# TensorE of a fused attention and expert kernel in periods of two slots

## The chip, the cores and the metric

The kernel runs on one core of one Trainium2 chip. The metric is the device time of that core in microseconds (us), the median of several executions. The profile is one further execution, taken by the hardware profiler; times in it count from the span's start.

## The reference, cut to what matters

The input x is [8, 256, 128] in float32. It is normalised over its last axis. One branch is causal attention with 16 heads of 64: queries from x, keys and values through a latent of 64, rotary positions, softmax, output projection. The other branch is a feed-forward network of 8 experts (128 to 512 to 128, GELU) of which each token takes one, and a SiLU behind it. The result is x plus attention times gate:

```python
q = q * cos + _rotate_half(q) * sin
k = k * cos + _rotate_half(k) * sin
scores = einsum('bhsd,bhtd->bhst', q, k) / sqrt(D) + causal
probs = softmax(scores)
out = einsum('bhst,bhtd->bhsd', probs, v)
s = out.reshape(B, S, H * D) @ wo.T
g = silu(2 * expert_of_token(xn))
return x + s * g
```

## The kernel before, in words

Attention goes by slots. A slot is a pair of heads of one batch: 8 slots a batch (NP), 64 slots in all, number g. Each engine has its own list of instructions, written out slot by slot by a function `slot(g)`, and the engines meet only at semaphores; every engine works strictly down its list. Between slots 39 and 40 (G_LEAD is 40) stands the expert phase, 22 tiles of 128 sorted tokens.

What each engine does in slot g, in its order:

- TensorE: `scores(g+2)` (two heads, each on 64 rows of the array, into one PSUM bank a head, lines 1116 and 1118); `project(m)` of one item, a group of four heads' queries (even m, lines 1090 to 1092) or keys (odd m, lines 1106 and 1107); `turn(g)`, six transposes of the probabilities (line 1128); `output(g-3)` (line 1156); in even slots `values(g-2)`, which serves two slots and has 64 columns of the array a head (lines 1142 and 1144). Slots 0 to 23 and a few others (ALONE) have a values step of their own.
- VectorE: `row_max(g+2)` (masks the scores and takes the row maximum, four instructions, line 602), `denominators(g+1)` (the reciprocals `rden`, line 609), its share of `scale(g+1)` (line 620), then sometimes `finalise` of a batch (lines 784 to 790), then `rotate(m)` (the products of the rotary rotation, line 593).
- ScalarE: the exponentials of g+1 (line 906), a copy of the context (`ctx_out`, line 935), the copies of the turned probabilities (`turned_probs(g)`, line 928), its share of `scale(g+1)` (line 919).
- GpSimd (POOL): its share of `scale(g+1)` (line 477), then the sum that ends a rotation (`rotated(m)`, line 466, into `staged`), then in slots 22 to 37 one `scatter` of 128 tokens to DRAM by expert (line 485), and in slots 43 to 58 one `gather` (line 493).
- SyncE starts transfers: `place(n)`, four moves from `staged` to `qk_sb` (line 366), when both items 2n and 2n+1 are summed; `store` of a finished batch; and in slot 38, once all scatters have landed, the loads of the sorted tokens into `z` (line 428). It also works down one list, and a wait in it holds back all that follows.

`items(g)` is the item projected, rotated and summed in slot g, g+6 up to slot 36, and TWICE puts a second one into slots 36 and 38, so that item 45 belongs to slot 38 and from slot 39 on it is g+8. Scores of a slot wait for their moves (`qk_in`) and for both heads' maxima of the slot before (`masked_ready`).

SyncE's slot, the lines that matter:

```python
if g == G_LEAD - 2:
    sp.wait_ge(scattered, 16 * NT)
    load(0, 4)
    sp.wait_ge(xs_in, 16)
    load(4, NR)
for m in items(g):
    if m % 2:
        place(m // 2)
```

TensorE ends attention before the experts with `output`, `values(39)`, a wait for the first load of `z` (`xs_in` 16), the first transpose of a tile of tokens (line 1297), `output(39)`; it waits for the second load (`xs_in` 32) before the second product of tile 1 (line 1339).

## Time and profile before

| | us |
|---|---|
| median of 3 runs | 305.51 (305.35 to 305.71) |
| the profiled execution, its own time | 305.23 |
| its span from first to last instruction | 303.5 |
| TensorE busy | 290.1 (96% of the span) |
| ScalarE busy | 243.2 (80%) |
| VectorE busy | 227.1 (75%) |
| GpSimd busy | 217.2 (72%) |

The profiled execution's time is its span and 1.7 us around it. Busy time of TensorE is modelled from pipelined matmuls, and a busy engine may also be one that works no faster than its supply comes. The shares are means over stages that have different limits.

### The profile page before, as it was taken

What the parts mean: (1) busy time and instruction counts of PE and PEld (TensorE: products, weight loads), DVE (VectorE), ACT (ScalarE), POOL (GpSimd) and SP (SyncE); (2) the same over time, 40 slices, a digit from 0 to 9 for tenths busy, and PEclk for the clock granted to TensorE, in tenths of its full rate; (3) what the DMA queues carried; (4) which work ended last, traced back from release to release, by engine and by line L of the source; (5) the groups of instructions that cost most, each with busy time, mean ns of one, the idle gap of its engine ahead of it and who ended that gap; (6) DMA issues with size and microseconds to landing.
All of it is one profiled execution on the core that took longest, in us unless ns stands there. A gap on an engine that the chain in (4) does not pass through costs nothing.

```text
span 303.5 us, 8596 instructions
## 1 busy us (share of the span) xinstructions
PE 290.1 (96%) x2362; PEld 234.8 (77%) x2362; DVE 227.1 (75%) x905; ACT 243.2 (80%) x871; POOL 217.2 (72%) x321
## 2 busy tenths in 40 slices
PE   8897999999999999999999999999999999899994
PEld 3665888888888888777777789999877777676763
DVE  4889998987786998988888524444398899897651
ACT  4387889898977789989898677777779989799982
POOL 3468878687777779999999963333158999899730
PEclk9999999999999999999999999999999999999999
DMA  6854594979433333333334490000513344344200
GB/s 203 251 132 116 104 297 116 236 172 303 101 68 65 67 77 83 101 88 98 89 88 109 96 288 6 2 2 0 154 38 83 100 120 117 93 115 123 61 19 17
DMA packets 39596, 33.35 MB, mean 110 GB/s; under 512 B 4801, under 2 KB 36674, under 8 KB 39554
## 3 DMA queue, kind: packets, MB, share of 16 engines
q1 hardware_dynamic: 38098, 30.51, 39.1%
q0 software_dynamic: 1024, 2.10, 2.5%
q8 instruction: 20, 0.33, 0.5%
q10 hardware_dynamic: 432, 0.23, 0.3%
q14 instruction: 22, 0.18, 0.2%
HBM read 11.07 MB, written 4.98 MB: 53 GB/s over the span
## 4 chain that ended last, share of the span: by engine, by line
PE 66%; POOL 12%; issue 8%; DVE 6%; DMA 3%; ACT 2%; SPq 2%; POOLq 1%; DVEq 0%; ACTq 0%
PE bank L1128 9%; PE bank L1116 9%; PE bank L1142 8%; PE bank L1339 7%; PE bank L1156 6%; PE bank L1327 6%; POOL probs L477 4%; POOL staged L466 4%; PE bank L1090 4%; PE bank L1144 3%; PE bank L1118 3%; DVE masked L602 2%; PE bank L1106 2%; POOL xn L493 2%; DMA z<-in_woT 2%
## 5 line engine op out<-in xcount | busy, mean ns | idle before, releaser
L906 ACT ACTIVATE pexp<-masked,negmax 128x128 f32<-128x128 f32 (+1 forms) x256 | 114.1, 453 | 2.2 <-DVE negmax L602 2.2
L477 POOL TENSOR_SCALAR probs<-pexp,rden 128x256 f32<-128x256 f32 (+1 forms) x184 | 80.3, 451 | 24.3 <-DVE rden L609 21.7
L602 DVE CUSTOM_DVE_ANT_0 masked<-bank,mask 128x128 f32<-128x128 f32 (+1 forms) x256 | 75.9, 352 | 25.2 <-PE bank L1118 25.0
L466 POOL TENSOR_TENSOR staged<-rot_out 128x512 f32<-128x512 f32 x63 | 80.1, 1273 | 17.5 <-DVE rot_out L593 16.9
L593 DVE TENSOR_TENSOR rot_out<-bank,rot 128x1024 f32<-128x1024 f32 x64 | 77.6, 1214 | 3.9 <-PE bank L1092 2.7
L928 ACT COPY probsT<-bank 128x384 f32<-128x384 f32 x128 | 55.0, 481 | 23.8 <-PE bank L1128 22.8
L1128 PE MATMUL bank<-ident,probs 128*128 128x128 f32 x384 | 54.1, 275 | 1.3 <-POOL probs L477 0.6
L906 ACT ACTIVATION_READ_ACCUMULATOR pexp<-masked,negmax 128x1 f32 x256 | 50.0, 195 | 0.0
L1116 PE MATMUL bank<-qk_sb 64*128 64x256 f32 x256 | 45.0, 427 | 3.2 <-DVE negmax L602 2.5
L1128 PEld LDWEIGHTS bank<-ident,probs 128*128 128x128 f32 x384 | 43.1, 140 | 4.1 <-issue 1.5
L1156 PE MATMUL bank<-vo_sb,ctxT 128*128 128x128 f32 x256 | 39.5, 279 | 0.7 <-ACT ctxT L935 0.7
L1142 PE MATMUL bank<-probsT,lat_all 128*64 128x256 f32 (+1 forms) x184 | 37.7, 488 | 0.3 <-ACT probsT L928 0.3
L1156 PEld LDWEIGHTS bank<-vo_sb,ctxT 128*128 128x128 f32 x256 | 33.6, 191 | 2.0 <-ACT ctxT L935 1.1
L1074 ACT ACTIVATE probsT<-bank,w_own 128x128 f32<-128x128 f32 x88 | 25.0, 369 | 12.7 <-PE bank L1327 12.7
L1116 PEld LDWEIGHTS bank<-qk_sb 64*128 64x128 f32 x256 | 19.4, 184 | 17.0 <-issue 14.2
L551 POOL COPY w_own<-w_sb 128x516 f32 x22 | 14.9, 678 | 23.1 <-ACT probsT L1074 22.9
L1118 PEld LDWEIGHTS bank<-qk_sb 64*128 64x128 f32 x256 | 25.1, 187 | 2.6
L935 ACT COPY ctxT<-bank 128x256 f32<-128x256 f32 (+1 forms) x46 | 20.7, 451 | 6.0 <-PE bank L1144 5.1
L1118 PE MATMUL bank<-qk_sb 64*128 64x128 f32 x256 | 25.0, 270 | 0.0
L885 DVE TENSOR_TENSOR z<-bank,b_all 128x128 f32 (+1 forms) x22 | 6.4, 292 | 24.2 <-PE bank L1339 21.7
L1144 PEld LDWEIGHTS bank<-probsT,lat_all 128*64 128x64 f32 x184 | 13.3, 137 | 14.3 <-issue 10.3
L1339 PE MATMUL bank<-w_sb,probsT 128*128 x176 | 23.3, 276 | 0.3 <-ACT probsT L1074 0.3
(114 smaller groups left out, 485.6 us busy)
## 6 DMA issues: line engine op xcount, KB each, us to landing
qk_sb<-staged SPq DMA_DIRECT2D x128, 128.0 KB, 2.7
w_sb<-in_w SPq DMA_DIRECT2D x2, 1024.0 KB, 6.1
w_sb<-in_w SPq DMA_DIRECT2D x4, 512.0 KB, 4.8
sorted_x<-z SPq DMA_DIRECT2D x1, 1408.0 KB, 8.0
sorted_g<-z SPq DMA_DIRECT2D x1, 1152.0 KB, 5.9
out<-res SPq DMA_DIRECT2D x8, 128.0 KB, 1.9
x_sb<-in_x SPq DMA_DIRECT2D x3, 256.0 KB, 3.3
rot<-in_c_rot SPq DMA_DIRECT2D x1, 512.0 KB, 5.8
```

Source lines behind the costliest of these rows:

```text
L466: pool.tensor_tensor(staged[:, n % 2, :, m % 2, :], rot_out[:, m % 2, :, 0:S], rot_out[:, m % 2, :, S:2 * S], op=ALU.add).then_inc(staged_ ...
L477: pool.tensor_scalar(probs[:, g % 2, i, c], pexp[:, g % 2, i, c], rden[:, g % 2, i, k:k + 1], 1.0, ALU.mult, ALU.mult).then_inc(probs_read ...
L593: dve.tensor_tensor(rot_out[:, m % 2], bank_of(m)[:].unsqueeze(1).broadcast_to([P, 2, 2 * S]), rot[:], op=ALU.mult).then_inc(rope_done, 1)
L602: t = dve.tensor_tensor_reduce(masked[:, g % 2, i, c], s_bank[i][:, c], mask[:, c], -1.0, -NEG * 1e8, ALU.add, ALU.min, negmax[:, g % 2, i ...
L906: e = act.activation(pexp[:, g % 2, i, c], masked[:, g % 2, i, c], ACT.Exp, bias=negmax[:, g % 2, i, k:k + 1], scale=-1.0, accum_out=rowsu ...
L928: act.copy(probsT[:, g % 4, i, :], t_bank[i][:, 0:SW]).then_inc(probsT_ready, 1)
L1116: pe.matmul(s_bank[i][:, P:SW], qk_sb[r, 0, p, P:S], qk_sb[r, 1, p, :], start=True, stop=True)
L1118: m = pe.matmul(s_bank[i][:, 0:P], qk_sb[r, 0, p, 0:P], qk_sb[r, 1, p, 0:P], start=True, stop=True)
L1128: t = pe.transpose(t_bank[i][:, k * P:(k + 1) * P], probs[:, g % 2, i, k * P:(k + 1) * P], ident[:])
L1142: pe.matmul(o[r, :, :], lat_all[:, 2 * b, :], probsT[:, pairs, i, 0:S], start=True, stop=False)
L1156: m = pe.matmul(y_bank[:, i * C:(i + 1) * C], ctxT[:, p, i * P:(i + 1) * P], vo_sb[:, p, :], start=(p == 0 and i == 0), stop=(p == NP - 1) ...
L1339: m = pe.matmul(bank[6 + i][:, 0:C], hidT[:, i, k, :], w2_sb[:, k, :, :].rearrange("p e c -> p (e c)")[:, bass.ds(e * C, C)], start=(k == ...
```

## The change

In slots 26 to 37 and 42 to 57 TensorE writes two slots as one period s (s even): `scores(s+2)`, `values(s-2)`, `scores(s+3)`, `turn(s)`, one projection, two outputs, `turn(s+1)`, the next projection. In these slots VectorE does the rotation of slot g-1's items, ahead of `denominators(g+1)`, and GpSimd sums them in slot g; ScalarE copies the context in even slots after both exponentials. TWICE moves from slots 36 and 38 to 22 and 24, so `items(g)` is g+8 from slot 25 on. SyncE's list is left as it was, but it follows `items(g)`. `staged_ready` becomes one semaphore for each parity of item, scores wait for each head's maxima by itself, and the finish of batch 5 goes from slot 51 to slot 50. The sums, scalings and moves stay on their engines.

```diff
--- before.py
+++ after.py
@@ -40,7 +40,7 @@
 
 LEAD = 5
 AHEAD = 6
-TWICE = (36, 38)
+TWICE = (22, 24)
 G_LEAD = LEAD * NP
 TURNS = ((0, 2), (2, 4), (4, 8), (8, 12), (12, 16))
 W_PARTS = NG
@@ -49,10 +49,12 @@
 SCATTER_SLOT = 22
 GATHER_SLOT = G_LEAD + 3
 GATHER_ORDER = (10, 11, 0, 1, 2, 3, 12, 13, 4, 5, 6, 7, 8, 9, 14, 15)
-FINALS = {48: 0, 51: 5, 53: 1, 54: 2, 56: 3, 59: 6, 61: 4}
+FINALS = {48: 0, 50: 5, 53: 1, 54: 2, 56: 3, 59: 6, 61: 4}
 FINAL_ORDER = tuple(FINALS.values()) + (7,)
 Z_PART = 18
 FIRST_DOUBLE = 3 * NP
+PERIODS = (*range(26, G_LEAD - 2, 2), *range(G_LEAD + 2, B * NP - 6, 2))
+SCATTERS = tuple(range(SCATTER_SLOT, SCATTER_SLOT + NT))
 ALONE = tuple(range(FIRST_DOUBLE)) + (G_LEAD - 2, G_LEAD - 1, B * NP - 2, B * NP - 1)
 
 
@@ -65,6 +67,20 @@
 
     ahead = [AHEAD + sum(t < n for t in TWICE) for n in (g, g + 1)]
     return range(g + ahead[0], min(g + 1 + ahead[1], B * NP))
+
+
+def in_period(g):
+
+    return g - g % 2 in PERIODS
+
+
+def rotations(g):
+
+    behind = items(g - 1) if in_period(g - 1) else []
+    return [*behind] if in_period(g) else [*behind, *items(g)]
+
+
+VECTOR_SUMS = ()
 
 
 def host_constants():
@@ -254,7 +270,7 @@
 
         proj_done = sem("proj_done")
         rope_done = sem("rope_done")
-        staged_ready = sem("staged_ready")
+        staged_ready = [sem(f"staged_ready{i}") for i in range(2)]
         qk_in = [sem(f"qk_in{p}") for p in range(NP)]
         scores_done = sem("scores_done")
         masked_ready = sem("masked_ready")
@@ -297,7 +313,7 @@
 
         def scaler(g, i, k):
 
-            busy = SCATTER_SLOT <= g - 1 < SCATTER_SLOT + NT or GATHER_SLOT <= g - 1 < GATHER_SLOT + NT
+            busy = g - 1 in SCATTERS or GATHER_SLOT <= g - 1 < GATHER_SLOT + NT
             if g == 0 or g >= B * NP - 3:
                 return ("vector", "pool")[i]
             return "pool" if k or not busy else ("vector", "scalar")[i]
@@ -358,7 +374,8 @@
         def _(sp):
             def place(n):
 
-                sp.wait_ge(staged_ready, 2 * n + 2)
+                for i in range(2):
+                    sp.wait_ge(staged_ready[i], n + 1)
                 wait(sp, scores_done, 2 * n + 2 - NP)
                 for pair in range(2):
                     p = 2 * (n % NG) + pair
@@ -464,7 +481,7 @@
                 for q in (2 * n - 4, 2 * n - 3) if n > 1 else ():
                     pool.wait_ge(qk_in[q % NP], 32 * (q // NP) + 32)
                 pool.tensor_tensor(staged[:, n % 2, :, m % 2, :], rot_out[:, m % 2, :, 0:S], rot_out[:, m % 2, :, S:2 * S],
-                                   op=ALU.add).then_inc(staged_ready, 1)
+                                   op=ALU.add).then_inc(staged_ready[m % 2], 1)
 
             def scale(g):
 
@@ -537,10 +554,12 @@
                     rstd(2 + g // 4)
                 if g == G_LEAD - 1:
                     first_weights()
-                for m in items(g):
-                    rotated(m)
-                if SCATTER_SLOT <= g < SCATTER_SLOT + NT:
-                    scatter(g - SCATTER_SLOT)
+                for m in rotations(g):
+                    if m not in VECTOR_SUMS:
+                        rotated(m)
+                for n in range(NT):
+                    if SCATTERS[n] == g:
+                        scatter(n)
                 if GATHER_SLOT <= g < GATHER_SLOT + NT:
                     gather(GATHER_ORDER[g - GATHER_SLOT])
 
@@ -589,9 +608,16 @@
             def rotate(m):
 
                 dve.wait_ge(proj_done, m + 1)
-                wait(dve, staged_ready, max(m - 1, 2) if m > 1 else 0)
+                wait(dve, staged_ready[m % 2], m // 2)
                 dve.tensor_tensor(rot_out[:, m % 2], bank_of(m)[:].unsqueeze(1).broadcast_to([P, 2, 2 * S]), rot[:],
                                   op=ALU.mult).then_inc(rope_done, 1)
+                if m == 1 or m in VECTOR_SUMS:
+                    n = m // 2
+                    dve.wait_ge(rope_done, m + 1)
+                    for q in (2 * n - 4, 2 * n - 3) if n > 1 else ():
+                        dve.wait_ge(qk_in[q % NP], 32 * (q // NP) + 32)
+                    dve.tensor_tensor(staged[:, n % 2, :, m % 2, :], rot_out[:, m % 2, :, 0:S], rot_out[:, m % 2, :, S:2 * S],
+                                      op=ALU.add).then_inc(staged_ready[m % 2], 1)
 
             def row_max(g):
 
@@ -744,9 +770,6 @@
                 dve.wait_ge(rot_in, 16)
                 rotate(0)
                 rotate(1)
-                dve.wait_ge(rope_done, 2)
-                dve.tensor_tensor(staged[:, 0, :, 1, :], rot_out[:, 1, :, 0:S], rot_out[:, 1, :, S:2 * S],
-                                  op=ALU.add).then_inc(staged_ready, 1)
                 normalise(1)
                 rotate(2)
                 turned_low(1)
@@ -777,6 +800,7 @@
 
             def finalise(b):
                 k = FINAL_ORDER.index(b)
+                wait(dve, res_ready, k)
                 dve.wait_ge(g_in[b], 32)
                 g2 = gate[:, 2 * b:2 * b + 2, :].rearrange("p n c -> p (n c)")
                 if b >= LEAD:
@@ -791,7 +815,7 @@
                                   op=ALU.add).then_inc(res_ready, 1)
 
             def slot(g):
-                if 0 < g // NP < LEAD and g % NP == (2 if NP * (g // NP) <= FIRST_DOUBLE else 3):
+                if 0 < g // NP < LEAD and g % NP == (2 if NP * (g // NP) <= FIRST_DOUBLE or in_period(g) else 3):
                     take_y(g // NP - 1)
                 if g in FINALS and FINALS[g] >= LEAD:
                     finalise(FINALS[g])
@@ -805,6 +829,9 @@
                     row_max(g + 2)
                 if g == G_LEAD + 1:
                     gate_rows(NR - 1, 1)
+                if in_period(g):
+                    for m in rotations(g):
+                        rotate(m)
                 if g + 1 < B * NP and g != G_LEAD:
                     denominators(g + 1)
                     scale(g + 1)
@@ -854,8 +881,9 @@
                     tile_experts()
                 if g in FINALS and FINALS[g] < LEAD:
                     finalise(FINALS[g])
-                for m in items(g):
-                    rotate(m)
+                if not in_period(g):
+                    for m in rotations(g):
+                        rotate(m)
 
             def finish(b):
                 if b == B - 1:
@@ -1036,10 +1064,12 @@
                     exponentials(g + 1, 0)
                 if g > 1 and g - 2 in ALONE and g not in (G_LEAD, G_LEAD + 1):
                     ctx_out(g - 2)
-                if g % 2 and g > 2 and g - 3 not in ALONE and g not in (G_LEAD + 1, B * NP - 1):
+                if g % 2 and g > 2 and g - 3 not in ALONE and g not in (G_LEAD + 1, B * NP - 1) and not in_period(g):
                     ctx_out(g - 3)
                 if more:
                     exponentials(g + 1, 1)
+                if g in PERIODS:
+                    ctx_out(g - 2)
                 if g == B * NP - 2:
                     ctx_out(g - 2)
                 if g == B * NP - 1:
@@ -1111,8 +1141,8 @@
 
                 p = g % NP
                 pe.wait_ge(qk_in[p], 32 * (g // NP) + 32)
-                wait(pe, masked_ready, 2 * g)
                 for i, r in enumerate(half_rows):
+                    wait(pe, masked_ready, 2 * g - 1 + i if g else 0)
                     pe.matmul(s_bank[i][:, P:SW], qk_sb[r, 0, p, P:S], qk_sb[r, 1, p, :], start=True, stop=True)
                 for i, r in enumerate(half_rows):
                     m = pe.matmul(s_bank[i][:, 0:P], qk_sb[r, 0, p, 0:P], qk_sb[r, 1, p, 0:P], start=True, stop=True)
@@ -1255,7 +1285,29 @@
                 pe.wait_ge(vo_ready, 2)
                 pe.wait_ge(lat_copied, 1)
 
+            def period(s):
+                scores(s + 2)
+                if s != G_LEAD + 2:
+                    values(s - 2)
+                scores(s + 3)
+                turn(s)
+                for m in items(s)[:1]:
+                    project(m)
+                if s - 2 not in PERIODS and s - 3 not in ALONE:
+                    output(s - 3)
+                output(s - 2)
+                output(s - 1)
+                turn(s + 1)
+                for m in items(s + 1):
+                    project(m)
+                for m in items(s)[1:]:
+                    project(m)
+
             def slot(g):
+                if in_period(g):
+                    if g in PERIODS:
+                        period(g)
+                    return
                 if g + 2 < B * NP:
                     scores(g + 2)
                 if g < 2:
@@ -1276,7 +1328,7 @@
                     turn_latents(g // 4)
                 if g == COUNT_SLOT:
                     count_tokens()
-                if g > 2 and g - 3 not in ALONE and g not in (G_LEAD, G_LEAD + 1, G_LEAD + 2):
+                if g > 2 and g - 3 not in ALONE and g not in (G_LEAD, G_LEAD + 1, G_LEAD + 2) and g - 2 not in PERIODS:
                     output(g - 3)
                 if g > 1 and g - 2 in ALONE and g not in (G_LEAD, G_LEAD + 1):
                     output(g - 2)
```

## Rows read from the trace of the kernel before

**Rows 1.** The page: busy time by engine, and the chain that ended last.

```profile
PE 290.1 (96%) x2362; PEld 234.8 (77%) x2362; DVE 227.1 (75%) x905; ACT 243.2 (80%) x871; POOL 217.2 (72%) x321
...
PE 66%; POOL 12%; issue 8%; DVE 6%; DMA 3%; ACT 2%; SPq 2%; POOLq 1%; DVEq 0%; ACTq 0%
```

**Rows 2.** Busy time of each engine in two stretches of attention.

```profile
core 0: us, PE busy (x) PEld busy (x) DVE busy (x) ACT busy (x) POOL busy (x), PEclk, DMA share, GB/s
...
132.60:160.30 27.70, 27.70 (x217) 21.59 (x217) 23.61 (x90) 25.36 (x92) 26.00 (x33) 1.00 0.37 97
...
232.20:257.90 25.70, 25.70 (x202) 19.83 (x200) 23.33 (x81) 23.82 (x89) 24.13 (x29) 1.00 0.42 106
```

**Rows 3.** Chain of waits, slots 29 and 30: start, us, what.

```profile
132.58 0.63 PE bank L1116 x4
...
134.11 0.66 PE bank L1128 x6
...
135.21 0.63 PE bank L1116 x4
...
136.06 0.31 PE bank L1090
136.38 0.12 PE bank L1091
...
138.07 1.01 PE bank L1142 x4
...
139.51 0.63 PE bank L1116 x4
```

**Rows 4.** Timeline of GpSimd, slots 28, 29 and 38: start, us, operation.

```profile
132.71 0.93 POOL L477 TENSOR_SCALAR probs<-pexp,rden 128x256 f32<-128x256 f32 x2
133.62 1.26 POOL L466 TENSOR_TENSOR staged<-rot_out 128x512 f32<-128x512 f32 x1
135.05 1.06 POOL L485 DMA_INDIRECT sorted_x<-xn,pos  x1 [0.17 <-issue]
136.15 0.93 POOL L477 TENSOR_SCALAR probs<-pexp,rden 128x256 f32<-128x256 f32 x2
...
168.44 1.62 POOL L477 TENSOR_SCALAR probs<-pexp,rden 128x128 f32<-128x128 f32 x4
170.04 2.51 POOL L466 TENSOR_TENSOR staged<-rot_out 128x512 f32<-128x512 f32 x2
```

**Rows 5.** SyncE's moves: timeline, line 366 alone, and issue to landing.

```profile
169.69 3.60 SPq L428 DMA_DIRECT2D z<-sorted_x  x2
...
L366 SPq DMA_DIRECT2D qk_sb<-staged x128: 590/608/2283, 12.2 to 278.6; - x128
...
z<-sorted_x SPq DMA_DIRECT2D x1, 256.0 KB, 2.8
z<-sorted_x SPq DMA_DIRECT2D x1, 0.5 KB, 7.0
```

**Rows 6.** Timeline of TensorE: first tile of the experts, second product of tile 1.

```profile
174.55 0.33 PE L1297 MATMUL bank<-ident,z 128*128 128x128 f32 x1
...
180.44 1.06 PE L1339 MATMUL bank<-w_sb,probsT 128*128 x8
```

**Rows 7.** Timeline of slots 42 and 43: VectorE's last mask, TensorE's turn, GpSimd's scaling.

```profile
226.75 0.82 PE L1128 MATMUL bank<-ident,probs 128*128 128x128 f32 x6
226.82 0.42 DVE L602 CUSTOM_DVE_ANT_0 masked<-bank,mask 128x256 f32<-128x256 f32 x1
...
230.73 1.00 POOL L477 TENSOR_SCALAR probs<-pexp,rden 128x256 f32<-128x256 f32 x2 [0.30 <-DVE rden L609]
```

**Rows 8.** VectorE's last step of a finish (min/median/max ns), and TensorE at slot 52.

```profile
L790 DVE TENSOR_TENSOR res<-gated,x_sb x8: 424/426/2118, 247.8 to 300.8; 128x256 f32<-128x256 f32 x8
...
259.30 0.70 PE L1116 MATMUL bank<-qk_sb 64*128 64x256 f32 x4 [1.19 <-DVE negmax L602]
```

**Rows 9.** Timeline of ScalarE, slots 29 and 30: copies of the turned probabilities.

```profile
134.53 0.86 ACT L928 COPY probsT<-bank 128x384 f32<-128x384 f32 x2 [0.43 <-PE bank L1128]
...
137.39 0.86 ACT L928 COPY probsT<-bank 128x384 f32<-128x384 f32 x2
```

**Rows 10.** Timeline of GpSimd and TensorE in slots 57 and 58.

```profile
280.14 0.94 POOL L477 TENSOR_SCALAR probs<-pexp,rden 128x256 f32<-128x256 f32 x2
280.84 0.87 PE L1128 MATMUL bank<-ident,probs 128*128 128x128 f32 x6
```

## The prediction

> **What bounds the kernel now.** I read the page first. TensorE is busy 96% of the span and the chain that ended last is 66% TensorE [rows 1], so the kernel looks bound by TensorE. Next come the stretches. In slots 29 to 36 GpSimd is busy 26.00 of 27.70 us, in slots 43 to 50 it is 24.13 of 25.70 [rows 2], and its timeline shows what the rest is: 0.17 us ahead of each scatter, no wait for anybody [rows 4]. One of its slots takes 136.15 - 132.71 = 3.44, two take 6.88. The chain gives TensorE 139.51 - 132.58 = 6.93 for two slots [rows 3]. So two engines are full at once, and TensorE has 0.05 us in two slots to win before GpSimd sets the pace. GpSimd's work from slot 22 to slot 38 is a fixed list: scalings, sums, scatters.
>
> Third, the end of that stretch. SyncE starts the load of the sorted tokens at 169.69; it lands 2.8 later, at 172.5, and only then the second load starts, which lands 7.0 later, at 179.5 [rows 5]. TensorE uses the first at 174.55 and the second at 180.44 [rows 6]. That leaves 2.05 and 0.9 us of slack. From there to 218 the expert tiles follow each other on TensorE, so what comes late here comes late at the end.
>
> **The change, part by part.**
>
> Fewer changes of the array's shape on TensorE. The first projection instruction after scores takes 0.31, its like behind it 0.12: 0.19 for a change from 64 rows to the full array. Scores behind another shape take 0.63 for their wide part; the narrow part, half as wide, takes 136.06 - 135.84 = 0.22, so 0.19 is the change. Values take 1.01 for the wide part and 139.51 - 139.08 = 0.43 for the half-wide one: 0.15 [rows 3]. Two slots have five changes now (scores, projection, scores, projection, values: 4 x 0.19 + 0.15 = 0.91), a period has four (scores, values, scores, turn: 0.72). A period is 6.93 - 0.19 = 6.74 us, and there are 14 periods, so at most 14 x 0.19 = 2.7 us. GpSimd's 6.88 leaves 14 x 0.05 = 0.7, and that only where TensorE, not GpSimd, ends the stretch. I take 0 in the sum.
>
> The second items move from slots 36 and 38 to 22 and 24. No sum stands in slot 26, and slot 38 sums items 45 and 46 as before. From slot 22 through 37 GpSimd has 17 sums in both kernels, so with no idle time it ends its last scatter and starts scale(39) at 168.44 and the sum of item 45 at 170.04, as now [rows 4]. The extra sums make it up to 2.5 us late in slots 24 to 26, which TensorE waits out and gets back by slot 38; cost 0. TensorE would reach the last turns about 1 us earlier, as slots 36 and 38 have one projection less; the next part takes this away.
>
> SyncE's list. This is the largest term. The move place(22) needs items 44 and 45. Item 45 was in slot 38, behind the loads of z. Now items(37) is 45, so place(22) stands in SyncE's slot 37, ahead of the loads; but the rotation is a slot late, so its sum is still in GpSimd's slot 38, behind scale(39). It ends at 170.04 + 2.51 / 2 = 171.30 [rows 4]. SyncE waits until then, issues four moves of 0.61 each [rows 5] and comes to the first load at 171.30 + 2.44 = 173.74 instead of 169.69: 4.05 late. It lands at 176.5, where TensorE used it at 174.55: 2.0 late. The second load starts then and lands at 176.5 + 7.0 = 183.5, where TensorE used it at 180.44: 3.1 late. If the second load takes only 6 us, with four competing moves fewer behind it, the first one decides: 2.0. I take 2.8, with 2.0 to 3.5 as bounds (the upper one for a first load slowed by the four moves ahead of it). Whoever is early before it gains nothing, and the expert phase behind has no slack on TensorE to take it back.
>
> The start of the second run of periods. In slot 42 no values step stands between scores(44) and scores(45), so scores(45) wait for VectorE's last mask, which ends at 226.82 + 0.42 = 227.24. With half the wide part and the narrow part (0.22 each) and the change of shape (0.19) turn(42) starts near 228.0 instead of 226.75 [rows 7]: 1.3 late. ScalarE has already copied the context by then (0.5 less to do), so the exponentials of 44, their reciprocals and scale(44) come 0.5 to 0.8 late; GpSimd was waiting for exactly those (0.30) [rows 7]. I take 0.5, with 0 and 1.2 as bounds.
>
> Rotation ahead of the reciprocals on VectorE. The products take 1.2 and now stand between row_max and `rden`. Behind `rden` wait GpSimd's scale and all the rest of its list. The working, by order of instructions: in a period of 6.88 the scores end 1.0 after its start, the masks 1.2 later, the products 1.2 later, so `rden(s+1)` is there at 3.6; GpSimd's scaling must end as turn(s+1) starts, at 6.74 - 0.48 - 0.66 = 5.6 and when GpSimd is full about 0.5 later (0.48 is the key projection, 0.66 from 134.11 on a turn [rows 3]), so it starts near 5.2: 1.5 us of slack where GpSimd is full. Just after slot 42, where TensorE is 1.3 behind, 0.2 to 0.4 is left. So this costs nothing while no finish stands in between. A finish is two steps of some 0.43 us, and its last step once took 2.12, beside GpSimd's work; TensorE then waited 1.19 [rows 8]. There are five finishes in slots 48 to 56. With less slack each can cost up to 0.8; or the bad one is gone and 1.2 comes back. I take 0.7, with -1.2 and +2.5 as bounds. The Trainium skill (SBUF — State Buffer, "The single rule") says that VectorE and GpSimd share one port pair as an exclusive lock, so that one of them blocks for a whole instruction. By that rule a finish beside a sum loses up to 1.3 us each time, and five would lose 6; the one long row in eight [rows 8] says it is rare.
>
> A sum owed. In slots 42 to 56 each sum is one slot later, so the sum of item 63 falls in slot 56, where GpSimd had none. It takes 1.26 [rows 4], and scale(58) stands behind it. That scaling is at 280.14 and turn(58) at 280.84 [rows 10], so they are tied. I take 0.8, with 0 and 1.3 as bounds.
>
> Waits by head: the first head's scores may start half a row_max early; -0.1. The split of `staged_ready`, the earlier finish of batch 5 and the extra wait on `res_ready`: 0, each is met long before.
>
> Sum: 2.8 + 0.5 + 0.7 + 0.8 - 0.1 = 4.7. The profiled execution takes 305.23, so 309.9; the median of the runs shown is 0.28 above it, and I predict 310.2.
>
> **Rivals.**
>
> Faster: the changes of shape decide. If TensorE alone set the pace in all 14 periods and the loads of z were not held back, 2.7 us would go: 302.8. Partly (first run as forecast here by GpSimd, second by TensorE) 304. For it speaks the 66% of TensorE in the chain; against it GpSimd without idle time, and the order of SyncE's list. It decides only if place(22) costs less than 0.9 us, that is if the sum of item 45 ends before about 168. The Trainium skill (TensorEngine Tiling (Array Packing), "Key Properties") says that a change of tiling mode drains the engine. It would make this rival's 2.7 us; it gives no price, and the trace agrees with 0.15 to 0.19 each.
>
> No change: the late load is hidden and the rest cancels. It would need TensorE to reach its first tile 2 us later than now for another reason. 305.5.
>
> Only SyncE's list costs: the first term stands, the others cancel. 308.3.
>
> ScalarE becomes the bound. values(s) now needs the copies of turn(s+1), which TensorE made just before it. ScalarE starts the copies 134.53 - 134.11 = 0.4 after a turn [rows 3, 9], the next ones 137.39 - 134.53 = 2.86 later, and they take 0.86 [rows 9]: done 4.1 after turn(s) began. TensorE comes to values(s) at 6.74 - 1.44 (values) - 0.86 (the second scores) = 4.44. That is 0.3 of slack, and the context's copy, 0.5 every second slot, is not in it; with 0.2 us lost in each of 14 periods 2.8 come on top: 313.0.
>
> **How the numbers follow.** Forecast (the late load and most of the small costs) 0.5; only the late load 0.24; ScalarE or VectorE as the bound on top 0.14; no change 0.04; faster 0.08. The likeliest case's own range is 308.8 to 311.6. The range that holds 8 in 10 takes the low bound of the first term with the rest near nothing, and the upper bounds of three of the four: 306.8 to 312.8. Within 0.2% (0.6 us, about what a measurement of this kernel can tell from no change) 0.04, faster 0.08, slower 0.88.
>
> **What would show it.** In the profile after: SyncE issues four moves between the end of GpSimd's first sum of slot 38 and the first load of z, and TensorE waits for that load ahead of its first line-1297 transpose, some 2 us. GpSimd's last scatter ends at the same time as before, within 1 us. A period takes 6.9, not 6.74. Scores(45) wait for the masks. Wrong would be: a last scatter well before 167, an expert phase that starts no later than 175, or periods of 6.7.

## The result, and the profile after

| | before | after |
|---|---|---|
| median of 4 runs, us | 305.61 (305.35 to 306.38) | 313.09 (310.41 to 316.04) |
| ratio | | 1.0211 (95%: 1.012 to 1.0303) |
| profiled execution, its own time | 305.23 | 316.04 |
| its span | 303.5 | 313.9 |

The medians differ by 7.5 us. The ratio leaves out the run of 316.04, which counts as a slow one, and by it the change costs 6.4 us. The four runs spread far more than those of before: 310.41, 311.56, 314.62 and 316.04, with mean granted clocks of 0.994, 0.993, 0.974 and 0.978. The profiled execution is the slowest of them, so its last landmarks overstate the difference by about 3 us.

The page of after, busy time and the chain by engine:

```profile
PE 296.2 (94%) x2362; PEld 240.6 (77%) x2362; DVE 227.9 (73%) x905; ACT 241.7 (77%) x871; POOL 218.4 (70%) x321
PE 68%; POOL 10%; DVE 9%; issue 7%; DMA 2%; ACT 2%; SPq 1%; POOLq 0%; DVEq 0%; ACTq 0%
```

Busy shares say nothing here: TensorE is busy for 6 us more and yet has a smaller share. The chain tells more, in order of time (start, us, what), from the last scatter to tile 1 of the experts:

```profile
168.19 1.01 POOL sorted_x L502
...
170.92 1.24 POOL staged L483
...
172.21 0.59 SPq L383
172.81 0.04 issue
172.85 0.61 SPq L383
173.46 0.04 issue
173.50 0.61 SPq L383
...
174.15 0.61 SPq L383
...
174.80 2.95 DMA z<-sorted_x
177.75 0.14 issue
177.89 0.45 PE bank L1349
```

GpSimd's sum of item 45, four moves issued by SyncE, the load of `z`, the first transpose of a tile: one chain, without a gap. The first load starts at 174.80 where it started at 169.69 [rows 5]. TensorE's own timeline for the same place (the brackets give the idle time ahead of a group and what ended it) and two stretches (busy time and count of TensorE, its weight loads, VectorE, ScalarE and GpSimd; then the granted clock):

```profile
177.89 0.45 PE L1349 MATMUL bank<-ident,z 128*128 128x128 f32 x1 [3.25 <-DMA z<-sorted_x]
...
179.19 1.92 PE L1379 MATMUL bank<-probsT,w_own 128*128 128x128 f32 x8
...
185.20 1.06 PE L1391 MATMUL bank<-w_sb,probsT 128*128 x8
```

```profile
133.36:160.27 26.91, 26.91 (x219) 21.42 (x218) 22.79 (x90) 24.68 (x93) 25.25 (x33) 1.00 0.34 87
177.90:184.47 6.57, 6.57 (x34) 6.57 (x35) 1.29 (x5) 2.29 (x8) 2.27 (x6) 0.55 0.76 209
```

Line 1349 is line 1297 of before, line 1391 is line 1339. The first transpose is 3.34 us later than in [rows 6], the second product of tile 1, which waits for the second load, 4.76. Behind the wait of 3.25 us TensorE runs at a granted clock of 0.55, the level of 1.2 GHz; the eight matmuls of line 1379 take 1.92 there.

The first line of the windows is four periods of the first run, 26.91 us. The chain gives their starts (wide part of the scores):

```profile
133.36 0.63 PE bank L1146 x4
...
140.09 0.63 PE bank L1146 x4
...
146.81 0.63 PE bank L1146 x4
...
160.27 0.63 PE bank L1146 x4
```

A period takes 6.73 us, where two slots took 6.93 [rows 3]. GpSimd's waits in the second run of periods, and its gathers around their end:

```profile
236.52 1.01 POOL L494 TENSOR_SCALAR probs<-pexp,rden 128x256 f32<-128x256 f32 x2 [2.51 <-DVE rden L635]
238.94 1.08 POOL L510 DMA_INDIRECT xn<-sorted_g,pos  x1 [0.17 <-issue]
...
262.37 1.02 POOL L494 TENSOR_SCALAR probs<-pexp,rden 128x256 f32<-128x256 f32 x2 [1.51 <-DVE rden L635]
...
270.57 1.02 POOL L494 TENSOR_SCALAR probs<-pexp,rden 128x256 f32<-128x256 f32 x2 [1.07 <-DVE rden L635]
...
283.96 1.04 POOL L510 DMA_INDIRECT xn<-sorted_g,pos  x1 [0.16 <-issue]
287.65 1.05 POOL L510 DMA_INDIRECT xn<-sorted_g,pos  x1 [0.16 <-issue]
```

Two finishing steps on VectorE, each beside GpSimd's work, and what follows on TensorE:

```profile
257.48 0.94 POOL L494 TENSOR_SCALAR probs<-pexp,rden 128x256 f32<-128x256 f32 x2
257.67 2.26 DVE L814 TENSOR_TENSOR res<-gated,x_sb 128x256 f32<-128x256 f32 x1
258.39 1.26 POOL L483 TENSOR_TENSOR staged<-rot_out 128x512 f32<-128x512 f32 x1
260.63 0.94 PE L1146 MATMUL bank<-qk_sb 64*128 64x256 f32 x3 [1.59 <-DVE negmax L628]
...
285.56 2.21 DVE L814 TENSOR_TENSOR res<-gated,x_sb 128x256 f32<-128x256 f32 x1
286.23 1.26 POOL L483 TENSOR_TENSOR staged<-rot_out 128x512 f32<-128x512 f32 x1
288.47 0.94 PE L1146 MATMUL bank<-qk_sb 64*128 64x256 f32 x3 [1.73 <-DVE negmax L628]
```

```profile
262.00:264.00 2.00, 2.00 (x12) 2.00 (x12) 1.66 (x11) 1.29 (x4) 1.64 (x3) 0.59 0.00 0
264.00:266.00 2.00, 2.00 (x13) 2.00 (x12) 1.44 (x3) 1.72 (x8) 1.68 (x2) 0.56 0.02 4
```

The rows show a sequence: a step that takes 0.4 to 0.8 us elsewhere is held until GpSimd's sum is done (it ends at 259.93, the sum at 259.65), the masks behind it are late, TensorE waits 1.59 us, and its clock then stands at 0.56 to 0.59 for 4 us. Before, this happened once, with a wait of 1.19 us [rows 8] and a granted clock of 1.00 behind it.

### The profile page after: what moved, and what is told of

Read it like the earlier page. It is cut to its first block, busy times and chain, and to the rows that moved or that the text cites. A ratio compares the mean times of both kernels' runs of the same rounds, so it can differ in the third digit from the quotient of the medians.

```text
span 313.9 us, 8604 instructions
## 1 busy us (share of the span) xinstructions
PE 296.2 (94%) x2362; PEld 240.6 (77%) x2362; DVE 227.9 (73%) x905; ACT 241.7 (77%) x871; POOL 218.4 (70%) x321
## 4 chain that ended last, share of the span: by engine, by line
PE 68%; POOL 10%; DVE 9%; issue 7%; DMA 2%; ACT 2%; SPq 1%; POOLq 0%; DVEq 0%; ACTq 0%
PE bank L1158 10%; PE bank L1146 9%; PE bank L1172 8%; PE bank L1379 7%; PE bank L1391 6%; PE bank L1186 6%; POOL staged L483 4%; DVE rot_out L612 3%; PE bank L1148 3%; PE bank L1120 3%; PE bank L1174 3%; DVE masked L628 3%; POOL probs L494 3%; POOL xn L510 2%; PE bank L1254 2%
## 5 line engine op out<-in xcount | busy, mean ns | idle before, releaser
L494 POOL TENSOR_SCALAR probs<-pexp,rden 128x256 f32<-128x256 f32 (+1 forms) x184 | 81.9, 460 | 32.3 <-DVE rden L635 28.3
L1158 PE MATMUL bank<-ident,probs 128*128 128x128 f32 x384 | 56.1, 280 | 0.7 <-issue 0.5
L1146 PE MATMUL bank<-qk_sb 64*128 64x256 f32 x256 | 48.1, 427 | 5.3 <-DVE negmax L628 5.1
L1172 PE MATMUL bank<-probsT,lat_all 128*64 128x256 f32 (+1 forms) x184 | 38.5, 496 | 0.3 <-ACT probsT L956 0.3
L1186 PE MATMUL bank<-vo_sb,ctxT 128*128 128x128 f32 x256 | 38.2, 284 | 0.5 <-ACT ctxT L963 0.5
L1146 PEld LDWEIGHTS bank<-qk_sb 64*128 64x128 f32 x256 | 21.3, 184 | 20.8 <-issue 16.7
L1148 PEld LDWEIGHTS bank<-qk_sb 64*128 64x128 f32 x256 | 26.8, 187 | 2.8
L1148 PE MATMUL bank<-qk_sb 64*128 64x128 f32 x256 | 27.9, 272 | 0.0
L1379 PE MATMUL bank<-probsT,w_own 128*128 128x128 f32 x176 | 25.1, 289 | 0.0
L1174 PEld LDWEIGHTS bank<-probsT,lat_all 128*64 128x64 f32 x184 | 14.0, 138 | 14.3 <-issue 10.3
```

Of the source, the lines that this page charges most:

```text
L494: pool.tensor_scalar(probs[:, g % 2, i, c], pexp[:, g % 2, i, c], rden[:, g % 2, i, k:k + 1], 1.0, ALU.mult, ALU.mult).then_inc(probs_read ...
L1146: pe.matmul(s_bank[i][:, P:SW], qk_sb[r, 0, p, P:S], qk_sb[r, 1, p, :], start=True, stop=True)
L1148: m = pe.matmul(s_bank[i][:, 0:P], qk_sb[r, 0, p, 0:P], qk_sb[r, 1, p, 0:P], start=True, stop=True)
L1158: t = pe.transpose(t_bank[i][:, k * P:(k + 1) * P], probs[:, g % 2, i, k * P:(k + 1) * P], ident[:])
L1172: pe.matmul(o[r, :, :], lat_all[:, 2 * b, :], probsT[:, pairs, i, 0:S], start=True, stop=False)
L1186: m = pe.matmul(y_bank[:, i * C:(i + 1) * C], ctxT[:, p, i * P:(i + 1) * P], vo_sb[:, p, :], start=(p == 0 and i == 0), stop=(p == NP - 1) ...
```

## The experiments

All are variants of the changed kernel if nothing else is said. Each was timed beside the kernel before on its chip; the ratios are to that. The median of the kernel before differs from chip to chip by up to 0.4 us (306.03 for runs 1 to 4, 305.68 for runs 5 to 8), so runs of different chips are compared by their ratios. Two traces of the same code can also stand up to 1 us apart at one place: the last product of the experts starts at 218.70 in the trace of the kernel before, at 219.65 in that of run 11, whose code is the same up to there.

**1. The load of `z` ahead of the moves of item 22.** The first term alone undone.

```diff
-                if g == G_LEAD - 2:
+                if g == G_LEAD - 3:
                     sp.wait_ge(scattered, 16 * NT)
                     load(0, 4)
```

> The changed kernel with the loads of z moved from SyncE's slot 38 to slot 37, ahead of place(22). If SyncE's order is the first term: the first load is issued within 1.5 us of the last scatter's end (near 170), TensorE waits for it less than 0.6 us, the expert phase ends 3 to 5 us earlier than the 222.8 of the changed kernel's profile, and the time falls by 3 to 6 us (the upper end if the half clock at the experts' start goes with the wait). Rival (the second run of periods and the owed sum carry the loss): less than 1.5 us.

Measured: 309.45 (308.69 to 311.53), ratio 1.0129 (1.0098 to 1.0161). Its load:

```profile
170.58 3.34 SPq L445 DMA_DIRECT2D z<-sorted_x  x2
```

The first transpose stands at 174.61, as before, and TensorE does not wait for it. The last product of the experts starts at 219.09, in the trace of the changed kernel at 223.52: 4.4 us come back there. In time it is 2.5 us by the ratios (1.0211 to 1.0129), with the wide interval of the changed kernel; runs 2 and 4 give a closer figure. Some 4 us stay lost, so the late load is the largest term and not the only one.

**2 and 3. One run of periods at a time.**

```diff
-PERIODS = (*range(26, G_LEAD - 2, 2), *range(G_LEAD + 2, B * NP - 6, 2))
+PERIODS = tuple(range(26, G_LEAD - 2, 2))            # run a2, FINALS with 51: 5
+PERIODS = tuple(range(G_LEAD + 2, B * NP - 6, 2))    # run a3, TWICE = (36, 38)
```

> Periods only in slots 26 to 37; slots 42 to 57 and the finish of batch 5 as in the kernel before. My theory gives the second run some 4 to 6 us of the loss (0.8 at its start, 1.9 at the finishes, 1.3 for the owed sum, the rest half clock in the tail), so the time is 4 to 6 us under the changed kernel. Rival (all of it is the late load): no more than 1 us under it.

> Periods only in slots 42 to 57, second items back in slots 36 and 38, so SyncE's list around the loads of z is as in the kernel before. Theory: the expert phase starts as in the kernel before (first line-1349 transpose at 174.5 to 175), and the time is 3 to 6 us over the kernel before, all of it behind slot 42. Rival (late load alone): within 0.6 us of the kernel before.

Measured: the first run with the late load 311.01 (310.67 to 311.12), ratio 1.0159 (1.0139 to 1.0178); the second run alone 307.75 (306.68 to 309.38), ratio 1.0046 (1.0027 to 1.0064). Both expectations missed: run 2 is 1.6 us under the changed kernel by the ratios (2.1 by the medians), not 4 to 6, and run 3 is 1.4 over the kernel before, not 3 to 6.

The trace of run 3 has the same held step and the same wait of TensorE as that of the changed kernel, with another clock behind them:

```profile
256.05 0.94 PE L1146 MATMUL bank<-qk_sb 64*128 64x256 f32 x3 [1.59 <-DVE negmax L628]
...
238.00:265.00 27.00, 25.41 (x200) 19.68 (x199) 23.29 (x86) 22.65 (x86) 24.09 (x30) 1.00 0.40 106
```

From the gather of slot 43 to that of slot 55 run 3 takes 43.56 us, the changed kernel's profiled execution 45.02, and run 1, where nothing was held in this stretch, 42.09. So the held step itself costs 1.5 us, and the half clock behind it, where it comes, about as much again.

**4. The first run of periods with the load first** (the edits of 1 and 2 together).

> Periods only in slots 26 to 37 and the loads of z ahead of place(22). Theory: GpSimd is full from slot 22 to 38 and sets the time of the last scatter, so periods on TensorE win little; but TensorE reaches the last turns about 1 us earlier, so the result is within 1.2 us under the kernel before (304.3 to 305.6). Rival (the changes of shape on TensorE pay): 6 periods of 0.19 on top, 303.2 or less.

Measured: 306.67 (306.24 to 307.55), ratio 1.0018 (1.0007 to 1.0029). The expectation, a time under the kernel before, missed, and its rival too. Runs 1 to 4 went on one chip, so their differences can be taken: the late load costs 311.01 - 306.67 = 4.3 us; the second run of periods 309.45 - 306.67 = 2.8, with some 1 us either way (run 1 spreads from 308.69 to 311.53); the first run wins nothing, although its periods are 0.2 us shorter. Run 3 puts the second run of periods at 1.4 only. Why the two figures differ is not shown; with periods in this stretch the times of a kernel spread more (2.7 to 3.3 us in runs 1, 3 and 7) than without them (0.4 to 1.3 in runs 2, 4, 11 and 12).

**5. Reciprocals ahead of the rotation.** With the edit of 1, VectorE's rotation goes from before `denominators(g + 1)` to the end of the slot.

```diff
-                if in_period(g):
-                    for m in rotations(g):
-                        rotate(m)
                 if g + 1 < B * NP and g != G_LEAD:
                     denominators(g + 1)
...
-                if not in_period(g):
-                    for m in rotations(g):
-                        rotate(m)
+                for m in rotations(g):
+                    rotate(m)
```

> Based on a1_load_first (309.45). In the periods VectorE makes the reciprocals and its scalings first and the rotation of slot g-1 last; sums still a slot late. If the rotation ahead of the reciprocals costs (third term, 1.5 to 2 us at the finishes): no wait of GpSimd for reciprocals over 0.6 us between the second gather and slot 57, and the time is 1.5 to 2.5 us under a1_load_first. Rival (the finishes stall wherever the reciprocals stand): within 0.6 us of a1_load_first.

Measured: 315.56 (315.06 to 317.39), ratio 1.0313 (1.0291 to 1.0334), some 6 us slower than run 1. The expectation was wrong. VectorE's timeline:

```profile
145.58 0.18 DVE L635 RECIPROCAL rden<-rowsum 128x4 f32<-128x4 f32 x1 [1.69 <-ACT pexp L930]
```

VectorE waits 1.69 us for the exponentials with nothing to do, and the rotation comes on top of that. Ahead of the reciprocals it fills this wait. That the rotation stands there is no cost: moved behind, it costs 5.6 us more by the ratios.

**6. Rotation at the end of its own slot** (`rotations(g)` becomes `items(g)`, same place as in 5, late load).

> The changed kernel with every rotation and its sum in its own slot again, behind the reciprocals; TensorE's periods, SyncE's code and the second items in slots 22 and 24 stay. Theory: the late rotation is behind the late load of z, the rotation ahead of the reciprocals and the owed sum, so all three go: the first load of z is issued before 171, and 5 to 7 us of the loss go, leaving 0 to +2 us over the kernel before (the missing values step at slot 42). Rival (TensorE's order itself costs): 309 or more.

Measured: 320.62 (319.82 to 322.23), ratio 1.0477 (1.0455 to 1.0499). Wrong as well: now VectorE waits for the projections, which a period has late. The view of waits from 125 to 160 (us in total, times, longest):

```profile
DVE rot_out L611 <- PE bank L1117: 7.6, 5, 1.7
```

The load of `z` starts at 176.30, later still. With these rotations at the end of their own slot the delay can't be had back; another place in the slot was not tried.

**7. Finishing steps out of the periods** (with the edit of 1).

```diff
-FINALS = {48: 0, 50: 5, 53: 1, 54: 2, 56: 3, 59: 6, 61: 4}
+FINALS = {50: 5, 58: 0, 59: 6, 60: 1, 61: 2, 62: 3, 63: 4}
```

> Based on a1_load_first. Only batch 5 is finished in the periods (slot 50); the six others from slot 58 on. If the finishes on VectorE cost inside the periods: the gathers of slots 43 to 55 take 12 x 3.45 = 41.4 plus at most 1.6 (one stall, slot 50), and the time falls by up to 1 us; the tail, where VectorE has room, takes the rest. Rival (port and order cost nothing): no change within 0.5 us, or slower by the finishes at the end.

Measured: 306.22 (305.49 to 308.77), ratio 1.0026 (1.0005 to 1.0048). The edit was worth 3.2 us by the ratios of runs 1 and 7 (some 1.2 either way), more than expected. The last step of the finishes, in run 1 and here (ns: least, median, most; first and last start):

```profile
L814 DVE TENSOR_TENSOR res<-gated,x_sb x8: 424/594/2201, 249.6 to 303.5; 128x256 f32<-128x256 f32 x8
```

```profile
L814 DVE TENSOR_TENSOR res<-gated,x_sb x8: 424/500/724, 253.8 to 301.6; 128x256 f32<-128x256 f32 x8
```

The step of 2.2 us is gone, with it TensorE's wait of 1.72 us behind it, and the granted clock stays at 1.00 to the end; in run 1 it was 0.85 from 284 to 290. But the held step is the smaller part of the 3.2 us. Run 8 below has the finishing steps where run 1 has them, and none was held in its trace (0.77 us at most). From the gather of slot 56 to the end of the span it still takes 25.73 us, run 1 26.23 and run 7 24.44. In this place TensorE waits 0.28 and 0.71 us in run 8 and 0.82 and 0.55 us in run 7, but only in run 8 the clock falls:

```profile
285.00:298.00 13.00, 11.96 (x74) 7.25 (x74) 6.24 (x38) 11.49 (x44) 7.41 (x13) 0.87 0.29 78
```

```profile
284.00:290.00 6.00, 5.94 (x42) 4.36 (x42) 4.79 (x24) 6.00 (x25) 4.33 (x9) 1.00 0.26 72
```

From 288 to 290 it is 0.51 in run 8, and a values step and its narrow part take 2.71 us there instead of 1.45. This is the 1.3 us between runs 8 and 7; run 1, with the held step, takes 0.5 more. Why the clock fell behind the shorter waits and not behind the longer ones is open.

**8. TensorE kept busy while it waits for the load** (late load).

```diff
                     pe.wait_ge(masked_ready, 2 * G_LEAD + 4)
+                    pe.wait_ge(rope_done, 47)
+                    keep_warm(14, bank[4])
                     pe.wait_ge(xs_in, 16)
```

> The changed kernel with 14 idle matmuls (bf16, 128 x 512, into a bank nobody reads) on TensorE ahead of its wait for the first load of z; output unchanged. If the half clock at the start of the experts is a price of the wait: the granted clock stays 1.00 from 175 to 184, the first expert matmuls take 0.9 instead of 1.7 us each eight, and the time is 1.5 to 2.5 us under the changed kernel's. Rival (the clock falls for another reason, or the wait alone costs): no change, or up to 0.5 us slower.

Measured: 313.31 (312.5 to 318.76), ratio 1.0259 (1.0221 to 1.0296), no gain; the rival was right.

```profile
174.71 3.19 PE L1254 MATMUL bank<-ones 128*128 128x512 bf16 x14
...
178.74 1.16 PE L1381 MATMUL bank<-probsT,w_own 128*128 128x128 f32 x8
...
185.03 1.15 PE L1393 MATMUL bank<-w_sb,probsT 128*128 x8 [1.11 <-issue]
```

The eight matmuls take 1.16 instead of 1.92 us, so the clock was kept. But the second product of tile 1 starts at 185.03 against 185.20: it waits for the second load. The profile names nobody for this wait of 1.11 us, but the load was issued at 177.95 and took 6.9 us to land, so it was there at 184.85; in the changed kernel 177.82 and 7.0 give 184.82. The half clock behind the wait for `z` costs nothing.

**9 and 10. Without the 16 gathers,** to see whether GpSimd's full list hides what the periods win. Both kernels leave out the gathers, so their last products use other data than the reference's; 9 is the kernel before, 10 the one of run 1.

```diff
-                if GATHER_SLOT <= g < GATHER_SLOT + NT:
-                    gather(GATHER_ORDER[g - GATHER_SLOT])
...
-                dve.wait_ge(g_in[b], 32)
+                dve.wait_ge(g_out, 32)
```

> The kernel before without the 16 gathers (the finishes multiply by the normalised tokens instead of the gates, so the output is another). GpSimd has 1.1 us less in each of slots 43 to 58. In slots 44 to 49 TensorE alone sets the pace: two slots take 6.93. Time 1 to 4 us under the kernel before.

> a1_load_first without the 16 gathers (same effect on the output). Rival under test, that the changes of shape on TensorE pay where GpSimd is not full: a period takes 6.73 in slots 44 to 49 against 6.93 for two slots in d1_before_no_gather. In time I expect it still 0 to 2.5 us over d1_before_no_gather: 8 x 0.2 = 1.6 won against 1 us at slot 42, the finishes and the owed sum, which costs nothing here because GpSimd has room.

Measured: 304.22 (304.15 to 304.82), ratio 0.9955 (0.9939 to 0.997), and 305.99 (305.55 to 306.88), ratio 1.0006 (0.9994 to 1.0017). With GpSimd relieved the periods are still 1.8 us behind. Two slots of 9 take 6.93 us, as with gathers, and a period of 10 takes 6.73 where no finish stands in it, so in the second run GpSimd's list is not what keeps the win of the periods away.

**11 and 12. Late finishing steps without the second run of periods.** 11 is the kernel before, with `FINALS = {51: 5, 58: 0, 59: 6, 60: 1, 61: 2, 62: 3, 63: 4}` and `finalise` waiting for the finish before it (`wait(dve, res_ready, k)`), as in the changed kernel. 12 is run 4 with the same `FINALS`.

> The kernel before, with five of its seven finishing steps that sit in slots 48 to 59 moved to slots 58 to 63, as in the run that took 3.2 us off the changed kernel. Theory A: the finishing steps cost most where VectorE has no room, in the periods of two slots, because there the whole item's reciprocals and the scaling behind them wait (1.51 and 1.07 us at two places of the changed kernel's trace). The kernel before has its own waits of 0.4 to 1.2 us there, so it gains little: 304.6 to 305.9, at most 1.0 us under the kernel before. Theory B: the placement is as poor in the kernel before, which would gain as much as the changed one: 302.3 to 303.2. Theory C: the tail, with seven steps behind slot 58, gets longer by more than the middle gains: 306.2 or more.

> The run with periods of two slots in slots 26 to 37 alone and with the first load ahead of the moves of item 22 (1.0018 of the kernel before), now with the finishing steps late as well. It stands against the run with both stretches of periods and late finishing steps (306.2, 1.0026). Theory A: with the finishing steps away, the second stretch of periods costs nothing or little more than its start in slot 42, 0.3 to 0.5 us: this run gives 305.4 to 306.1. Theory B: the second stretch still costs what it cost before, 2.8 us: 303.3 to 303.9. Theory C: the second stretch wins by its shorter periods (seven periods by 0.2 us): this run comes out above 306.6.

Measured: 304.97 (304.75 to 305.34), ratio 0.9972 (0.9962 to 0.9983), and 305.01 (304.8 to 305.17), ratio 0.9975 (0.9964 to 0.9986). Both beat the kernel before, by 0.9 and 0.8 us by the ratios; no other version with the same output does. Theory A holds for the first: the kernel before gains 0.9 where the changed one gained 3.2. The second lies between A and B: once the finishes are out of its way, the second run of periods costs 1.6 us by the ratios of runs 7 and 12 and 1.2 by their medians. Where that is, the gathers show, of run 12 and then of run 7 (slots 43, 55 and 56):

```profile
234.13 1.08 POOL L510 DMA_INDIRECT xn<-sorted_g,pos  x1 [0.16 <-issue]
...
276.17 1.04 POOL L510 DMA_INDIRECT xn<-sorted_g,pos  x1 [0.16 <-issue]
278.36 1.03 POOL L510 DMA_INDIRECT xn<-sorted_g,pos  x1 [0.17 <-issue]
```

```profile
235.21 1.08 POOL L510 DMA_INDIRECT xn<-sorted_g,pos  x1 [0.17 <-issue]
...
276.75 1.04 POOL L510 DMA_INDIRECT xn<-sorted_g,pos  x1 [0.16 <-issue]
280.16 1.04 POOL L510 DMA_INDIRECT xn<-sorted_g,pos  x1 [0.16 <-issue]
```

From slot 43 to 55 the periods win: 41.54 us against 42.04, 0.5. From slot 55 to 56 they take 3.41 against 2.19: 1.2 lost where the owed sum stands, of which 0.4 comes back by the end of the span. At the gather of slot 43 run 7 is 1.1 behind, but 0.6 of it is already there at the end of the experts, where both kernels have the same code. Counted from the first scores behind the experts, the gather of slot 43 comes after 14.43 us in run 7 and after 13.97 in run 12. All traces give this figure to 0.01, 14.42 or 14.43 with the second run of periods (after, 1, 3, 7, 8) and 13.97 or 13.98 without it (before, 2, 4, 11, 12): the start costs 0.45.

## Why the prediction was right, and where its terms were off

Right were the side and the mechanism of the largest term. Its size was not: 4.3 us, above its own upper bound of 3.5. The median is 2.9 us above the forecast and 0.3 above the stated range. By the ratio the time is 1.0211 x 305.6 = 312.1, within it by 0.7. With runs that spread over 5.6 us it is partly luck on which side of 312.8 the result falls. The lower end has a slip of its own: 305.5 and the first term's 2.0 give 307.5, not 306.8.

| term | forecast | measured |
|---|---|---|
| load of `z` held back by SyncE's list | 2.8 (2.0 to 3.5) | 4.3 (2 less 4); 4.4 in the traces of after and 1, at the end of the experts |
| first run of periods | 0 | 0.1 (12 less 11) to 0.6 (4 less before) |
| start in slot 42 | 0.5 (0 to 1.2) | 0.45 at the first gather, in all traces |
| rotation order and finishes | 0.7 (-1.2 to 2.5) | 1.8, some 1.3 either way: (1 less 7) less (4 less 12) by the ratios, 3.2 - 1.3 |
| owed sum | 0.8 (0 to 1.3) | 1.2 (7 less 12, slots 55 to 56) |
| periods of the second run | 0 | -0.5 (7 less 12, slots 43 to 55) |

**The late load.** The mechanism is as forecast: run 1 undoes it alone, and runs 2 and 4 give its size. This was off at several places. The sum of item 45 ended at 172.13, not 171.30: 0.28 of this was already there before slot 22, 0.56 is a wait of GpSimd for `rden` in slot 27, behind the second items of slots 22 and 24, which the forecast costed at nothing because TensorE catches up. TensorE did; GpSimd's list could not, for it had no idle time in it. The four moves took 0.65 each with the gap between them, not 0.61. So the load started 5.1 late instead of 4.05. And TensorE's wait is not the first load's (3.3 late) but the second's, 4.8 at the product of tile 1, as run 8 shows: the forecast had 2.0 and 3.1 for the two and took 2.8 between them, where the later one decides.

**Period length.** "A period takes 6.9" was wrong, and periods of 6.7, which the forecast named as a sign against itself, were there. It took 6.73, as the arithmetic of the shape changes had it (6.74). The stated reason, that GpSimd sets the pace at 6.88, does not hold within the run: TensorE came 2 to 3 us behind out of slots 22 to 26 (its turn of slot 27 starts 3.1 us later than before, that of slot 35 1.9) and ran at its own pace while it caught up, and GpSimd stayed as it was. That the first run wins nothing was right, and for the reason given: its end hangs on GpSimd's list. In the second run the periods do win 0.5 us of a possible 7 x 0.2, and the two ends of the run cost more.

**Start in slot 42.** The working has small slips: 227.24 + 0.22 + 0.22 + 0.19 is 227.87, which is 1.1 late and not 1.3. Counted from the first scores behind the experts, turn(42) came 1.4 later than before (8.45 against 7.06 us), scale(44) 1.0 later and the first gather 0.45. The 0.5 in the sum was right.

**Rotation ahead of the reciprocals.** This step was half wrong. Its title named the order; run 5 shows that the order saves some 6 us. The second half of the same step, the finishes, is the cost: run 7 against run 1. The working had it as "with less slack each can cost up to 0.8; or the bad one is gone". In the profiled execution two of eight last steps took 2.2 us, in runs 1 and 3 one, in run 8 none. Each brings a wait of 1.6 to 1.7 us on TensorE, and with it, in three cases of four, a stretch at half clock, which the forecast had not priced. Its size shows from slot 43 to 55: 42.09 us without a held step (run 1), 43.56 with one (run 3), 45.02 with one and the half clock (after). The stretch behind slot 56 has the half clock without a held step too (run 8). This would also explain the two groups of after's four runs, near 311 at a clock of 0.994 and near 315 at 0.976; it is argued from the clocks, since only one of the four left a trace.

The Trainium skill (SBUF — State Buffer, "The single rule") has VectorE and GpSimd block each other for whole instructions. The rows of after agree in this: both held steps, begun at 257.67 and 285.56, ended 0.28 us behind GpSimd's sum. The other six took 0.42 to 0.66 us, but beside four of them it was GpSimd's scaling that took longer, 0.63 to 0.72 us at a median of 0.47. What the rows don't explain is why a held step was not let in between GpSimd's scalings and its sum.

**The rivals.** "Only the late load", 308.3, is refuted by run 1, in which 3.9 us remain without it (ratio 1.0129). "Faster" fell with its condition: the sum of item 45 ended at 172.13, not before 168. Run 4, without the late load and without the second run, is no faster either. ScalarE as the bound is not seen: inside the first run TensorE has no idle time in 26.91 us. "No change" needed a TensorE that is late by itself, and it waited 3.25 us.

**What the forecast named as signs.** Four moves between the sum and the load: seen. A TensorE wait of some 2 us: 3.25. Last scatter within 1 us: 0.86 later. Scores(45) behind the masks: seen (TensorE waits 0.84 us for them), and scale(44) waits 2.51 us where it waited 0.30 [rows 7].

Open stays where the 0.6 us of run 4 over the kernel before are, since the traces of one code differ by more; why the second run of periods costs 1.4 us in run 3 and 2.8 in run 1 less run 4; and what decides whether the clock falls. That the finishes cost run 4 (1.3 us by the ratios) more than the kernel before (0.9) is within the noise.

## What to carry to other kernels

When a step is moved by a slot on one engine, follow it into the queue that works down a fixed list behind it: here four transfers that became due one slot earlier and ready one slot later held back a load that the whole next phase waited for, and one line gave 4.3 us back. A local win (0.2 us a period, really there) must be followed to the end of its stretch and set against the entry and exit of the new order; here these two cost more than all periods won. And before giving an engine's slack away, look for the rare long instruction in its rows (2118 ns at a median of 426 [rows 8]): with less slack it comes through. It was not held more often here (none to two of eight steps with periods, one of eight without), but a held step cost TensorE a wait of 1.6 to 1.7 us with periods and at most 1.2 without.

## What the runs showed of the hardware

- The granted clock fell from 1.00 to 0.55, the level of 1.2 GHz, behind a wait of TensorE of 3.25 us. Behind a wait of 1.59 us it fell to 0.56 to 0.59 for some 4 us in the changed kernel and stayed at 1.00 in run 3, so the length of the wait alone did not decide; behind one of 1.19 us in the kernel before it stayed at 1.00 too. With fourteen matmuls in place of the long wait it stayed up.
- An addition of 128x256 on VectorE with both inputs in SBUF took 424 to 500 ns in most cases and 2.1 to 2.26 us in some beside a scaling and a sum of GpSimd, in none, one or two of the eight cases of a run. One such step moved the end of its stretch by 1.5 us, and by 2.9 us with the half clock behind it.
- Leaving one change of the array's shape out of five made a pair of slots 0.20 us shorter (6.73 against 6.93), in both runs of periods.
